# Routing by blocks of rows, and an output stored in two parts, in a graph and mixture-of-experts kernel

## The chip, the cores and the metric

One core of a Trainium2 chip. The number is device time in microseconds of one execution, start to end. The kernel before was run three times: 926.48, 929.12 and 930.1 us, median 929.12. All profile rows come from one more execution, with the profiler on.

## The reference

625 rows of 768 numbers pass two graph convolutions, then one transformer layer whose feed-forward part is a mixture of 8 experts, of which each row uses its best. All in float32. The part that this change touches, cut down:

```
x2   = x + attention(...) @ Wp + bp
h2   = layernorm(x2) * g + b
gate_logits = h2 @ Wg                       # 625 x 8
w, sel = top_k(gate_logits, 1)              # softmax over one value: w = 1
hid  = relu(h2 @ W1[sel] + b1[sel])         # 768 -> 3072
y    = hid @ W2[sel] + b2[sel]              # 3072 -> 768
out  = x_in + (x2 + w * y)
```

## The kernel before

**Rows and slots.** The 625 rows stand as C = 5 blocks of P = 125 rows on the partitions. Each expert takes CAP = 128 slots; a row's slot is 128 times its expert plus its rank among the rows of that expert (`own`), where rank is a count of the rows before it with the same choice. Rows beyond the 128 of an expert go to overflow tiles (`far`, `kk`, `home`, `over`), which a loop at the end runs if there are any.

**Precision.** Each float32 operand is split in a high part, written by ScalarE (`split_hi`, tile `whi`; helper line L599), and a low part, the difference, written by VectorE (`split_lo`, tile `wlo`; helper line L894). A product is three products.

**Weights.** W1 and W2 of an expert come in SCH = 16 chunks of 1152 KB: FCH = 8 of W1, 8 of W2. SyncE loads them into RAWS = 4 buffers `raw`; a buffer is free once the low part of its chunk is made. `whi`/`wlo` have SLOTS = 4 buffers, free once TensorE has used the chunk (`s_used`).

**The router.** For each block c: TensorE projects (`rows_product`), VectorE adds the residual (x2) and norms (n2), TensorE transposes n2, ScalarE scales it to h2T, TensorE makes the 8 gate products (L1596). The gates of block c-2 are made behind the projection of block c. When all five are there (`s_gate`), VectorE works on all blocks at once: best gate and its index, one-hot marks `ohb`/`ohe` (L1158 to L1173); TensorE counts ranks and totals with 20 small products (L1619, L1622); VectorE, having made the low part of chunk 0 ahead of that, computes `own`, the marks `oh0` of expert 0's rows (L1206), then slots and overflow tables (up to L1228). TensorE picks expert 0's rows with 60 products of marks and n2 into PSUM (L1639). ScalarE scales them (`hgf`, L819) and makes `hgh`, VectorE `hgl`, and the first expert starts. `keep_busy` issues products whose result nobody reads, 24, 24, 50 and 24 of them here.

**Tokens by DMA.** POOL scatters the five blocks of n2 to `hs_d` in DRAM by their slots (L548), then loads each expert's 128 rows one expert ahead (`next_in`, L554). Expert 0's own rows don't take this way. `hTT`, the hidden layer turned, lies over n2, so in expert 0 ScalarE and VectorE wait for the scatters at k = 7 (k - 2 = OVER_N2).

**One expert** (`tile`, chunks k = 0 to 15): products of W1 (L1675), ScalarE reads them (`hid`), TensorE transposes them, VectorE adds b1 (`bia`, L1258), ScalarE and VectorE make the two parts of relu (`hTT`); then products of W2 (L1694) into PSUM banks 4 and 5. At W2 chunk 1 the next expert's rows are transposed. Each expert's y is copied to `ysb` and POOL stores it to `ys_d` (L559).

**The last expert and the end.** The rows of experts 0 to 6 come back from `ys_d` with five gathers (`y_back`, L563), issued when TensorE has used 10 chunks of the last expert, and are added to `base` (L1279). The last expert's y takes no DMA: its marks `oh7T` and the one-hot choice `oh8T` were transposed in expert 0 (`marks_turned`); TensorE adds b2 by products with `oh8T` (`bias_y`, L1710) and spreads the split y over the rows with `oh7T` (`spread_y`, L1715), VectorE adds each block (L1289), and SyncE stores it (L456).

**Order.** All five engines run lists written out by hand; what stands behind a waiting instruction of an engine waits with it.

## Time and profile before

| what | value |
|---|---|
| median of three runs | 929.12 us |
| the profiled execution | 930.92 us |
| its span, first to last instruction | 929.4 us |
| TensorE busy | 874.0 us, 94% of the span |
| VectorE busy | 705.7 us, 76% |
| ScalarE busy | 556.4 us, 60% |
| POOL busy | 90.3 us, 10% |
| moved by DMA | 196.01 MB, 211 GB/s over the span |

The span runs from the first to the last instruction; the profiled execution's own time is 1.52 us more. Busy shares are averages over stages with different limits, so the stages are read by windows. Times inside the trace count from the span's start. In the chain of waits each line is a piece of work that the end depended on.

### The profile page before, as it was taken

What the parts mean: (1) busy time and instruction counts of PE and PEld (TensorE: products, weight loads), DVE (VectorE), ACT (ScalarE), POOL (GpSimd) and SP (SyncE); (2) the same over time, 40 slices, a digit from 0 to 9 for tenths busy, and PEclk for the clock granted to TensorE, in tenths of its full rate; (3) what the DMA queues carried; (4) which work ended last, traced back from release to release, by engine and by line L of the source; (5) the groups of instructions that cost most, each with busy time, mean ns of one, the idle gap of its engine ahead of it and who ended that gap; (6) DMA issues with size and microseconds to landing.
All of it is one profiled execution on the core that took longest, in us unless ns stands there. A gap on an engine that the chain in (4) does not pass through costs nothing.

```text
span 929.4 us, 14804 instructions
## 1 busy us (share of the span) xinstructions
PE 874.0 (94%) x5460; PEld 842.0 (91%) x5460; DVE 705.7 (76%) x1060; ACT 556.4 (60%) x780; POOL 90.3 (10%) x88
## 2 busy tenths in 40 slices
PE   7999898989998888899889999999999999999998
PEld 7899897989998667689889989999999999999996
DVE  7997155784333899855559889898998989898895
ACT  5503223154323788842548778787887878787870
POOL 2000006031000400012050000000000000000041
PEclk9999788999999999999799999999999999999998
DMA  7020006348114910060189999999999999999984
GB/s 228 3 101 1 1 2 119 85 101 183 55 51 112 326 71 2 1 185 1 36 254 327 331 349 354 376 335 377 363 361 377 354 378 344 379 358 368 369 288 130
DMA packets 116008, 196.01 MB, mean 211 GB/s; under 512 B 33828, under 2 KB 83196, under 8 KB 115958
## 3 DMA queue, kind: packets, MB, share of 16 engines
q1 hardware_dynamic: 107796, 169.08, 54.7%
q0 software_dynamic: 6336, 24.19, 7.8%
q10 hardware_dynamic: 1826, 2.06, 0.8%
q8 instruction: 33, 0.54, 0.2%
q14 instruction: 17, 0.14, 0.0%
HBM read 177.40 MB, written 17.90 MB: 210 GB/s over the span
## 4 chain that ended last, share of the span: by engine, by line
PE 43%; DVE 29%; DMA 13%; issue 7%; ACT 7%; SPq 0%; DVEq 0%; ACTq 0%
DVE wlo L894 14%; PE ps L1323 13%; DMA raw<-in_L_ffn_W 12%; PE ps L1499 7%; PE ps L1675 5%; PE ps L1694 5%; ACT whi L599 3%; DVE pr L1094 2%; DVE hTT L892 2%; DVE pTl L894 2%; PE ps L1352 1%; PE ps L1559 1%; DVE pr L1101 1%; DVE ohs L945 1%; DMA xs<-in_x 1%
## 5 line engine op out<-in xcount | busy, mean ns | idle before, releaser
L894 DVE TENSOR_TENSOR wlo<-raw,whi 128x2304 fp32r<-128x2304 f32 x137 | 350.9, 2570 | 23.7 <-ACT whi L599 23.5
L599 ACT ACTIVATE whi<-raw 128x2304 fp32r<-128x2304 f32 x139 | 296.2, 2132 | 83.4 <-DMA raw<-in_L_ffn_W 34.3
L1694 PE MATMUL ps<-whi,hTT 128*128 128x384 f32 x768 | 201.6, 339 | 1.0 <-ACT oh7T L599 1.0
L1694 PEld LDWEIGHTS ps<-whi,hTT 128*128 128x128 f32 x768 | 139.2, 188 | 1.2 <-ACT oh7T L599 1.2
L1675 PE MATMUL ps<-whi,hgh 128*128 128x384 f32 x384 | 134.1, 349 | 2.8 <-DVE hgl L894 2.8
L1675 PE MATMUL ps<-whi,hgl 128*128 128x384 f32 x384 | 130.3, 339 | 0.0
L1675 PE MATMUL ps<-wlo,hgh 128*128 128x384 f32 x384 | 129.8, 338 | 0.0
L1694 PE MATMUL ps<-wlo,hTT 128*128 128x384 f32 x384 | 129.0, 336 | 0.0
L1675 PEld LDWEIGHTS ps<-whi,hgh 128*128 128x128 f32 x384 | 73.3, 191 | 2.9 <-DVE hgl L894 2.9
L1675 PEld LDWEIGHTS ps<-wlo,hgh 128*128 128x128 f32 x384 | 73.2, 191 | 0.0
L1675 PEld LDWEIGHTS ps<-whi,hgl 128*128 128x128 f32 x384 | 73.0, 190 | 0.0
L1694 PEld LDWEIGHTS ps<-wlo,hTT 128*128 128x128 f32 x384 | 72.3, 188 | 0.0
L1352 PE MATMUL ps<-ohd,ohs 125*125 125x314 bf16 x400 | 58.2, 304 | 7.7 <-DVE ohd L946 5.7
L1352 PEld LDWEIGHTS ps<-ohd,ohs 125*125 125x125 bf16 x400 | 53.8, 139 | 10.9 <-DVE ohd L946 9.0
L1258 DVE TENSOR_TENSOR bia<-ps,b1T 128x384 f32<-128x384 f32 x64 | 35.6, 556 | 16.2 <-PE ps L1662 16.2
L606 ACT ACTIVATE root<-var 125x2 f32<-125x2 f32 (+2 forms) x13 | 2.7, 204 | 67.0 <-DVE var L914 66.9
L894 DVE TENSOR_TENSOR ql<-ps,qh 64x125 fp32r<-64x125 f32 (+1 forms) x66 | 21.8, 331 | 26.5 <-ACT qh L599 25.4
L1536 PE MATMUL ps<-ident,pr 125*125 125x125 f32 x168 | 30.6, 300 | 12.1 <-DVE pr L1101 7.6
L1536 PEld LDWEIGHTS ps<-ident,pr 125*125 125x125 f32 x168 | 22.4, 189 | 20.5 <-DVE pr L1101 9.5
L892 DVE SCALAR_TENSOR_TENSOR hTT<-bia,hTT 128x384 fp32r<-128x384 f32 x64 | 35.5, 554 | 5.6 <-ACT hTT L599 5.6
L599 ACT ACTIVATE qh<-ps 64x125 fp32r<-64x125 f32 (+1 forms) x66 | 20.1, 305 | 31.9 <-PE ps L1499 23.0
L756 ACT ACTIVATE pr<-pr,negmax 125x126 f32<-125x126 f32 (+4 forms) x60 | 36.0, 600 | 2.2 <-DVE negmax L1094 1.5
(282 smaller groups left out, 1761.6 us busy)
## 6 DMA issues: line engine op xcount, KB each, us to landing
raw<-in_L_ffn_W SPq DMA_DIRECT2D x128, 1152.0 KB, 6.9
hs_d<-bc POOLq DMA_DIRECT2D x13, 384.0 KB, 6.3
raw<-in_L_gnn_W SPq DMA_DIRECT2D x4, 1152.0 KB, 6.4
hs<-hs_d POOLq DMA_DIRECT2D x8, 384.0 KB, 5.6
ys_d<-ysb POOLq DMA_DIRECT2D x7, 384.0 KB, 6.0
raw<-in_L_ffn_Wv SPq DMA_DIRECT2D x6, 384.0 KB, 5.8
raw<-in_L_ffn_Wq SPq DMA_DIRECT2D x6, 384.0 KB, 5.2
raw<-in_L_ffn_Wk SPq DMA_DIRECT2D x6, 384.0 KB, 6.0
```

What stands on the lines that cost most here:

```text
L599: act.activation(out_, in_, func).then_inc(s, 1)
L756: act.activation(pr[:, u % PRS, 0:n], pr[:, u % PRS, 0:n], ACT.Exp, bias=negmax[:, u % 4, :], scale=-1.0, accum_out=ssum[:, u // 2 % 2, u ...
L892: dve.scalar_tensor_tensor(out_, in_, 0.0, hi_, ALU.max, ALU.subtract).then_inc(s, 1)
L894: dve.tensor_tensor(out_, in_, hi_, ALU.subtract).then_inc(s, 1)
L1094: dve.tensor_tensor_reduce(pr[:, u % PRS, 0:n], score_rows(u)[:, 0:n], cmask[:, (C - 1 - c) * P:(C - 1 - c) * P + n], -(float(D) ** -0.5), ...
L1258: dve.tensor_tensor(bia[:, k % 2, :, :], blocks(2 + k % 2, 128, JW, CAP), bcol.rearrange("p (j o) -> p j o", o=1).broadcast_to((128, JW, C ...
L1323: ins = mm(ps[0:P, bank + half, 0:HB], l, rr, start=m == 0 and i == 0, stop=m == DC - 1 and i == 2)
L1352: ins = mm(ps[0:P, m, 0:HALF], ohs[:, i % EU, m * P:(m + 1) * P], ohd[:, i % EU, :], start=i in BOUNDS, stop=i + 1 in BOUNDS)
L1499: ins = mm(ps[:, 2 * (m % 2) + half, 0:HALF], l, rr, start=c == 0 and i == 0, stop=c == DC - 1 and i == 2)
L1536: ins = nc.tensor.transpose(turned_part(u)[:, b, :], pr[:, u % PRS, b * P:(b + 1) * P], ident[0:P, 0:P])
L1675: ins = mm(ps[0:CAP, k % 2, 0:FW], l, rr, start=m == 0 and j == 0, stop=m == DC - 1 and j == 2)
L1694: ins = mm(ps[0:CAP, 4 + half, 0:HB], l, rr, start=k == 0 and j == 0 and jj == 0, stop=k == FCH - 1 and j == JW - 1 and jj == 2)
```

## The change

What it does:

- *Router by blocks.* Gates, choice, ranks and marks of block c are made as soon as that block is ready, in the gaps of the others (`chosen`, `placed`, `ranks`, `choice`). The gates of block c-2 stand in the middle of the projection of block c. Expert 0's rows are picked block by block, in six separate banks, and go through ScalarE and VectorE in halves. The fillers are 40, 8 and 30. On ScalarE h2T of block c-1 comes before the root of block c, and split 0 before the last h2T.
- *Later steps.* Totals, overflow tables and slots come behind the first two splits; `slot1`, `slot2`, the exponential and the overflow counts at k = 10 of expert 0.
- *b2 by gathers.* POOL gathers each row's b2 from DRAM into `x2` (three gathers before the scatters of n2, two behind), VectorE adds it to `base` at k = 11 to 15 of expert 0. The transposed marks and the bias products are gone.
- *The output in two parts.* In expert 0, `base` of the last expert's rows is scattered into 128 slots (`bs_d`; the others' index is out of bounds and skipped) and loaded into `bc[1]`; small products with the marks give each slot's row number and weight (`last_rows`). Gathers of y start after 8 chunks of the last expert. SyncE stores all blocks without the last expert's y. At the end VectorE makes y * w + base for the 128 slots, and one indirect DMA writes them over their rows in the output; empty slots are skipped.

The diff, cut (semaphores, tensors and the overflow branch are left out):

```diff
-Y_BACK_AT = 10
+Y_BACK_AT = 8
-TURN_BUSY = 24
-CHOICE_BUSY = 50
+NORM_BUSY = 40
+GATE_BUSY = 8
+SPLIT_BUSY = 30
...
@@ sync
-                sp.wait_ge(s_fin, c + 1)
+                sp.wait_ge(s_yin, c + 1)
...
@@ gpsimd
+            def bias_rows(c):
+                g.wait_ge(s_oh8, 2 * c + 1)
+                g.wait_ge(s_n2, c + 1)
+                g.wait_ge(s_base, c + 1)
+                g.indirect_dma_start(out=x2[:, c, :], out_offset=None, in_=b2[:, :],
+                                     in_offset=bass.IndirectOffsetOnAxis(ap=eidx[:, c:c + 1], axis=0)
+                                     ).then_inc(s_b2g[c], 16)
+            for c in range(C):
+                g.wait_ge(s_x2, c + 1)
+                gp.tensor_tensor(base[:, c, :], base[:, c, :], x2[:, c, :], ALU.add).then_inc(s_base, 1)
+                if c >= 2:
+                    bias_rows(c - 2)
...
             g.wait_ge(s_scat, 16 * C)
             next_in(0)
+            g.wait_ge(s_slot7, 1)
+            for c in range(C):
+                g.wait_ge(s_base2, c + 1)
+                g.indirect_dma_start(out=bs_d[:, :], out_offset=bass.IndirectOffsetOnAxis(ap=slot7[:, c:c + 1], axis=0),
+                                     in_=base[:, c, :], in_offset=None, bounds_check=CAP - 1, oob_is_err=False
+                                     ).then_inc(s_b7sc, 16)
+            g.wait_ge(s_b7sc, 16 * C)
+            g.dma_start(bc[1][0:CAP, :], bs_d[:, :]).then_inc(s_b7, 16)
...
+            g.wait_ge(s_row7, 1)
+            g.wait_ge(s_out, 32 * C)
+            g.wait_ge(s_y7, 2)
+            g.indirect_dma_start(out=out[:, :], out_offset=bass.IndirectOffsetOnAxis(ap=row7[:, 0:1], axis=0),
+                                 in_=ysb[0:CAP, :], in_offset=None, bounds_check=N - 1, oob_is_err=False
+                                 ).then_inc(s_out7, 16)
...
@@ vector
+            normed_rows(0)
+            normed_rows(1)
+            chosen(0)
+            normed_rows(2)
+            chosen(1)
+            normed_rows(3)
+            chosen(2)
+            normed_rows(4)
+            d.wait_ge(s_iotac, 1)
+            placed(0, 3)
+            chosen(3)
+            placed(3, 4)
+            chosen(4)
+            placed(4, 5)
             split_lo(0, 0)
+            for i, part in enumerate((slice(0, HALF_IN), slice(HALF_IN, DC))):
+                d.wait_ge(s_hgh, i + 1)
+                lo(hg[1][:, part, :], hgf[:, part, :], hg[0][:, part, :], s_hgl)
+            split_lo(1, 0)
+            d.wait_ge(s_rank, C + 1)
...
+                    if first and k == FCH + 2:
+                        for c in range(C):
+                            dve.tensor_scalar(oh0[:, c, :], iotac[:, :], float(CAP * (E - 1)), home[:, c:c + 1],
+                                              ALU.add, ALU.is_equal).then_inc(s_ohe, 1)
...
+                    if first and FCH + 3 <= k < FCH + 3 + C:
+                        c = k - FCH - 3
+                        dve.scalar_tensor_tensor(base[:, c, :], x2[:, c, :], wtok[:, c:c + 1], base[:, c, :],
+                                                 ALU.mult, ALU.add).then_inc(s_base2, 1)
...
             for half in range(2):
...
-                lo(wlo[0][0:CAP, part], ps[0:CAP, 4 + half, 0:HB], whi[0][0:CAP, part], s_yl)
+                dve.scalar_tensor_tensor(ysb[0:CAP, part], ps[0:CAP, 4 + half, 0:HB], rowf[:, 1:2], bc[1][0:CAP, part],
+                                         ALU.mult, ALU.add).then_inc(s_y7, 1)
...
@@ tensor
-                rows_product(q, 2 * WP, c, 4 + 2 * (c % 2), None if c else {DC - 1: (s_pvl, 2 * STEPS)}).then_inc(s_wp, 1)
-                if c >= 2:
-                    gate_products(c - 2)
+                rows_product(q, 2 * WP, c, 4 + 2 * (c % 2), None if c else {DC - 1: (s_pvl, 2 * STEPS)},
+                             (lambda b=c - 2: gate_products(b)) if c >= 2 else None).then_inc(s_wp, 1)
                 if c >= 1:
                     turn_n2(c - 1)
+                if c >= 2:
+                    ranks(c - 2)
+            pe.wait_ge(s_x2, 4)
+            busy(NORM_BUSY, 7)
+            gate_products(3)
+            turn_n2(4)
+            busy(GATE_BUSY, 7)
+            pe.wait_ge(s_x2, C)
+            choice(0, range(2, DC))
+            ranks(3)
+            choice(1, range(2, DC))
+            gate_products(4)
+            choice(2, range(2, DC))
+            for c in range(3):
+                choice(c, range(2))
+            ranks(4)
...
+            choice(3, range(DC))
+            choice(4, range(DC)).then_inc(s_hgT, 1)
+            pe.wait_ge(s_rkread, C)
+            busy(SPLIT_BUSY, 3)
...
-                    if first and k == 1:
-                        marks_turned()
-                if first:
-                    pe.wait_ge(s_ohl, 2)
-                else:
+                if not first:
                     pe.wait_ge(s_yev, 2 * t)
...
-            def bias_y(c, half):
...
-            def spread_y(c, half):
```

## Rows read from the trace of the kernel before

**Rows 1.** windows of three stretches: length, PE, PEld, DVE, ACT, POOL busy, clock, DMA
```profile
449.50:452.50 3.00, 2.03 (x18) 1.94 (x18) 0.00 (x0) 2.14 (x7) 0.00 (x0) 1.00 0.00 0
452.50:455.00 2.50, 2.40 (x13) 2.40 (x13) 0.00 (x0) 2.48 (x3) 0.00 (x0) 0.56 0.00 0
...
535.00:545.00 10.00, 8.12 (x40) 7.80 (x39) 7.50 (x4) 7.04 (x5) 0.54 (x1) 0.83 1.04 376
...
655.00:709.00 54.00, 53.85 (x322) 53.25 (x321) 49.24 (x35) 43.80 (x42) 1.08 (x2) 1.00 1.03 364
```

**Rows 2.** chain of waits: start us, length us, what ran
```profile
...
475.22 8.09 PE ps L1675 x36
...
531.42 6.96 DMA raw<-in_L_ffn_W
...
541.51 4.71 PE ps L1675 x18
...
895.22 18.72 PE ps L1694 x108
...
```

**Rows 3.** timeline of TensorE in the router: start, length, operation
```profile
...
444.38 1.37 PE L1596 MATMUL ps<-wg,h2T 128*125 128x8 f32 x12
...
464.14 6.92 PE L1639 MATMUL ps<-oh,n 125*128 125x128 f32 x60
...
```

**Rows 4.** timeline of VectorE in the router
```profile
...
444.58 0.96 DVE L1146 TENSOR_TENSOR x<-ps,xfb 125x768 f32<-125x768 f32 x1 [4.05 <-PE ps L1323]
...
448.08 0.68 DVE L931 TENSOR_SCALAR n<-x,mv,rstd 125x768 f32<-125x768 f32 x1
...
461.35 1.07 DVE L1206 TENSOR_SCALAR oh<-iotac,rt 125x128 f32<-125x128 f32 x5
...
463.93 0.17 DVE L1217 CAST slot<-rt 125x5 int32<-125x5 f32 x1
...
465.09 5.01 DVE L894 TENSOR_TENSOR wlo<-raw,whi 128x2304 fp32r<-128x2304 f32 x2
...
```

**Rows 5.** timeline of ScalarE in the router
```profile
...
471.10 2.20 ACT L819 ACTIVATE hgf<-ps,lnT 128x128 f32<-128x128 f32 x6 [9.58 <-PE ps L1639]
473.33 0.84 ACT L599 ACTIVATE hgh<-hgf 128x768 fp32r<-128x768 f32 x1
...
```

**Rows 6.** timeline of SyncE, first weights after the router
```profile
...
460.48 18.70 SPq L442 DMA_DIRECT2D raw<-in_L_ffn_W  x4
...
```

**Rows 7.** timeline of VectorE in W1 chunks of a later expert
```profile
...
659.53 2.55 DVE L894 TENSOR_TENSOR wlo<-raw,whi 128x2304 fp32r<-128x2304 f32 x1
...
662.93 2.55 DVE L894 TENSOR_TENSOR wlo<-raw,whi 128x2304 fp32r<-128x2304 f32 x1
...
```

**Rows 8.** timeline of VectorE at the end
```profile
...
906.14 0.95 DVE L894 TENSOR_TENSOR hgl<-hgf,hgh 128x768 fp32r<-128x768 f32 x1
...
924.82 1.02 DVE L1289 SCALAR_TENSOR_TENSOR base<-ps,wtok,base 125x768 f32<-125x768 f32 x1 [1.54 <-PE ps L1715]
...
```

**Rows 9.** timeline of POOL behind the router and at the end
```profile
...
465.10 6.15 POOL L548 DMA_INDIRECT hs_d<-n,slot  x1 [17.48 <-DVE slot L1217]
...
476.52 3.31 POOL L548 DMA_INDIRECT hs_d<-n,slot  x1 [0.30 <-issue]
489.36 0.61 POOL L554 DMA_DIRECT2D hs<-hs_d  x1 [9.53 <-DMA hs_d<-n,slot]
...
895.59 3.08 POOL L563 DMA_INDIRECT x<-ys_d,slot  x1 [33.60 <-issue]
...
907.61 1.20 POOL L563 DMA_INDIRECT x<-ys_d,slot  x1 [0.31 <-issue]
...
```

**Rows 10.** page, costliest groups: busy, mean ns, idle before and its releaser
```profile
...
L1694 PE MATMUL ps<-whi,hTT 128*128 128x384 f32 x768 | 201.6, 339 | 1.0 <-ACT oh7T L599 1.0
...
```

**Rows 11.** landing of DMAs touching hs_d, then of the gathers into x2
```profile
DMA to landing us min/median/max: 2.7/6.3/12.6
...
DMA to landing us min/median/max: 6.6/7.9/8.5
```

More of the change, by code:

```diff
@@ L571, in _ @@
                 y_out(t)
[L572 removed]
+            g.wait_ge(s_base2, C)
             g.wait_ge(s_route, 1)
@@ L843, in tile @@
                         y_read(t)
-                    if k + AHEAD < SCH and not (first and k == 0):
+                    if k + AHEAD < SCH:
                         split_hi(k + AHEAD, t)
@@ new lines, in placed @@
+            def placed(c0, c1):
+                d.wait_ge(s_rank, c1)
+                d.wait_ge(s_oh8, 2 * c1)
+                dve.tensor_tensor(prod[:, c0:c1, :], rank8[:, c0:c1, :], ohe[:, c0:c1, :], ALU.mult
+                                  ).then_inc(s_rkread, c1 - c0)
+                d.wait_ge(s_rkread, c1)
+                step(dve.reduce_sum(rank[:, c0:c1], prod[:, c0:c1, :], AX))
+                step(dve.scalar_tensor_tensor(own[:, c0:c1], ef5[:, c0:c1], float(CAP), rank[:, c0:c1],
+                                              ALU.mult, ALU.add))
+                for c in range(c0, c1):
+                    dve.tensor_scalar(oh0[:, c, :], iotac[:, :], own[:, c:c + 1], None, ALU.is_equal).then_inc(s_oh0, 1)
@@ L1260, in tile @@
                                           ALU.add).then_inc(s_bia, 1)
-                    if k + 2 < SCH and not (first and k < 2):
+                    if k + 2 < SCH:
                         split_lo(k + 2, t)
@@ L1597, in gate_products, with ranks, choice, busy @@
                              start=m == 0, stop=m == DC - 1)
-                return ins
+                ins.then_inc(s_gate, 1)
+            ohb = rt[:, 4, 0:C * E // 2].bitcast(BF16).rearrange("p (c e) -> p c e", e=E)
+            def ranks(c):
+                pe.wait_ge(s_oh8, 2 * c + 1)
+                if c >= 3:
+                    pe.wait_ge(s_rkread, c)
+                for b in range(c + 1):
+                    ins = mm(ps[0:P, 3, c * E:(c + 1) * E], before[:, :] if b == c else onesb[:, :], ohb[:, b, :],
+                             start=b == 0, stop=b == c)
+                ins.then_inc(s_rank, 1)
+            def choice(c, part):
+                pe.wait_ge(s_oh0, c + 1)
+                for m in part:
+                    ins = mm(first_in(m), n2[:, c, m * 128:(m + 1) * 128], oh0[:, c, :], start=c == 0, stop=c == C - 1)
+                return ins
+            def busy(n, bank):
+                keep_busy(n, onesb[:, :], onesb[:, :], bank)
             pe.wait_ge(s_wg, 16)
```

322 lines of the change are left out of this document (152 added, 170 removed).

## The prediction

> **What bounds the kernel now.** I read the page first: TensorE is busy 94% of the span (the table above), so time can only come out of stretches where it works without need, waits, or runs at its lower clock. The table of windows finds them. Between 655 and 709 us one expert fills TensorE (53.85 of 54.00 us) while the DMA engines are busy too (364 GB/s), VectorE 49.2: a balanced stage which this change doesn't shorten. Around 450 to 475 it is different: TensorE is busy 2.03 of 3.00 us, and in the next 2.50 us its granted clock is 0.56, nearly the lower of its levels, 1.2 in place of 2.4 GHz [rows 1]. There the router works. The chain of waits shows three places: the router up to the first expert product at 475.22, waits on weight transfers around the start of expert 1 (one of 6.96 us; one group of 18 products at 541.51 takes 4.71 us where 3.13 is usual), and, from the last expert product's end (895.22 + 18.72 = 913.94) to 929.4, a tail of 15.5 us [rows 2].
>
> **The change, part by part.**
>
> *Router.* In before, the last block's projection ends at 444.4 and the experts start at 475.22: 30.8 us [rows 2, 3]. New chain, from the same moment. One gate group of 1.37 us [rows 3] now stands inside the last projection, and three tiny rank products before it (estimate 0.5): projection ends 446.2. x2 and norm take 4.2 (444.58 to 448.76); ScalarE now does six h2T (2.2 us, as its six of 471.10 in the same form) before the root, which holds it back an estimated 0.4: n2 of the last block ready at 451.0 [rows 4, 5]. Meanwhile TensorE does 40 fillers and gates of block 3, then the six transposes: 452.5. h2T 2.2 (the first whi split, 2.15, now fits ahead of it): 454.7. Gate products 1.4: 456.1 [rows 3, 5]. VectorE picks one block in six small steps of about 0.2: 457.5. Five rank products 0.6, then product, sum, own, one mark: 0.9, at 459.0. Choice products are 6.92/60 = 0.115 each; 24 to 36 of the 60 (blocks 0 to 2) are done in the gaps, the last 12 cost 1.4: 460.3 [rows 3]. ScalarE's half of the tile is half of 2.20 + 0.84, so 1.5: 461.8; VectorE's half 0.5: 462.3 [rows 4, 5]. With semaphore gaps I take 463.0, **12.2 us earlier**. Gone are the totals' arithmetic before the marks, the five marks in a row (1.07), the split of chunk 0 standing ahead of the rank reading (2.55) and most of the 50 fillers. Bounds: 462.3, if the clock stays up; 466, if gates, ranks and choices run at 1.2 GHz as the gates of 452.5 to 455 did [rows 1]. Fewer and shorter pauses speak for the full clock; I take nothing for it but 0.7.
>
> *Given back in expert 0.* The move of work past VectorE's queue has a price. Split 0 now ends at 461.6, about 1.1 later than the first weight issue shows in before (460.48) [rows 6]. Split 1 (2.55) follows the tile's lower half, at 466.4; the ten steps up to `slot` (about 2.1) follow; splits 2 and 3 end at 471.0 and 473.5. Chunk 1 then starts 0.8 late and chunk 2 1.2 late: **+2.0**. In the first eight chunks VectorE has a split of 2.55 and two instructions of half a us, overlapping a little, every 3.4 us, all that TensorE's pace leaves, so it regains nothing [rows 7]. Behind k = 10 come 5 marks and some 17 small steps, 3.5 us (0.17 each and half as much between dependent ones; five marks took 1.07 [rows 4]); at k = 12 four steps, 0.8; at k = 11 to 15 five base adds of 1.0 [rows 8]: 9.4 us. VectorE's slack in W2 chunks is 3.12 - 2.55 = 0.6 each, and it comes in with a lead of about one. Step by step: split 12 ends 505.2, then 3.5 of marks; split 13 511.3, chunk 13 wants it at 510.6 (0.7); split 14 514.9 (0.5 more); split 15 519.3 (1.3); expert 1's first split 525.9 (3.5). Net TensorE waits **+6.0**. Bounds: 1 (VectorE's lead is a full ring, about 5 us) and 9.4.
>
> *Scatter of tokens.* `slot` is ready at 468.4, not 464.1. I read the POOL rows against VectorE's: the issue of 895.59 ends at 898.67 and that of 476.52 at 479.83, each 1.1 us behind the end of a `wlo` split, while 471.56 and 907.61, with VectorE idle, take 1.2; the first, 6.15 us, ended 1.1 us behind a pair of splits without a gap [rows 4, 9]. In the new place VectorE splits every 3.4 us, so five issues end about 485, and 5.4 to 9.5 us later (from 479.83 to 489.36 it was 9.5) the rows have landed: 490 to 494. ScalarE waits for them at k = 7, which is now at about 491; the hid read behind that wait holds TensorE: **+1.5**, bounds 0 and 5. The three b2 gathers ahead of it lie beside the norms and cost nothing; if POOL were not free by 468 they'd delay the scatter, but each has 8 us. The base scatter and its load come at 505 to 530, and POOL's next work is the y of expert 0, stored after its end: hidden.
> The Trainium skill ("SBUF — State Buffer", Who interferes with whom) says that a VectorE tensor_tensor with both inputs in SBUF blocks GpSimd's reads for the whole instruction; the rows agree. The same skill ("GPSIMD Engine Reference", Instruction dispatch) would put the 6.15 us down to a code load of about 6 us at a first call; then the b2 gather would pay it, the scatters would end about 3 us sooner, and the +1.5 would be 0. The ends 1.1 us behind splits fit the first rule better.
>
> *Taken out of expert 0 and 1.* Ten transposes of marks (1.1), the wait for oh7T at the first W2 chunk (1.0 [rows 10]) and two ScalarE copies; one of the 1.7 us that chunks 0 and 1 took longer (36 in 8.09 where 6.3 is usual), since 30 fillers now bridge the gap ahead; and the waits on transfers with the low clock in them at 535 to 545, 1.9 idle and 1.7 [rows 1, 2]: TensorE now waits for VectorE in that place instead, and a later TensorE finds the weights there. Together **-6.7**.
>
> Last expert product's end: 913.9 - 12.2 + 2.0 + 6.0 + 1.5 - 6.7 = **904.5**. From expert 2 on nothing moves but the start.
>
> *Tail.* Gone: 20 bias products, 20 spread products, the splits of y, five final adds and the stores behind the last of them (924.82 + 1.02 to 929.4: 3.6) [rows 8]. Gathers start at chunk 8 of the last expert, 8 x 3.12 = 25 us before its end instead of 18.3; at 3.1 to 3.4 an issue the last ends 9.4 before the end and lands about 5.4 later [rows 9, 11], so at -4. VectorE's adds go from -6.8 (906.14 + 0.95 in before) to -1.9, SyncE's stores follow, the last lands 3.6 later: **+1.7**, so the stores don't quite hide. POOL's last scatter waits for them; y of half 1 is ready at +0.8 (0.25 + 0.5). Then 0.3 for POOL, 1.2 to issue (VectorE idle), landing: plain POOL stores show 2.7, the quickest gather 6.6, both from the issue's start [rows 11]; 78 of 125 rows, nothing beside it: 4.7. Tail 1.7 + 0.3 + 4.7 = 6.7, with the drain 7.0 instead of 15.5: **-8.5**. Bounds: 4.7 and 1.7 + 0.3 + 12.6 = 14.6 (the slowest landing).
> The Trainium skill ("DMA: Bandwidth & Descriptors", Anatomy of one DMA) fits a POOL DMA as 2.0 us plus bytes over 436 GB/s, an estimate of 2.6 for 0.24 MB; by it the tail would be nearer 5.
>
> Span 904.5 + 7.0 = 911.5. The profiled execution took 930.92 for a span of 929.4, so 913.0; the median of the runs shown is 1.8 below that execution. Forecast **912** (rounded up from 911.2 for the gaps between small steps).
>
> **Rivals.**
> A. *Weights set the end* (11 in 100). 124 transfers of 1152 KB come after the first freed buffer, at 350 to 365 GB/s where TensorE needs 350. If their stream has no slack, what counts is the first split, which is 1.1 us later: end at 915.0, tail 7.0, span 922.0, time **922**. For it: waits on `raw` in experts 0 and 1. Against: from 655 on TensorE has none.
> B. *The tail isn't shortened* (9 in 100): gathers that contend with the last weights, stores and then a dependent scatter in series, 15 us together as now. 904.5 + 15.5: **920**. For it: the +1.7 above; against: nothing else uses the DMA engines then.
> C. *POOL is kept out by VectorE* (5 in 100), the slower side. If each issue misses every gap as the first did, 6.15 + 0.3: token scatters end at 502, land at 508 or later, expert 0 stands 15 us instead of 1.5 (end at 918); the five gathers end at +7, land at +12.4, stores at +17, the last scatter at +29: span 947, time **947**. It decides from about 4.2 us an issue. Against: of the ten issues only that one missed a gap between two splits.
> D. *No move*: VectorE's added 9.4 falls whole on TensorE, clock at 1.2 GHz in the router, scatter +5: 904.5 + 3.4 + 3 + 3.5 = 914.4, tail 12, span 926.4: **926** (3 in 100).
>
> **How the numbers follow.** Forecast 72 in 100, its own range 904 to 919. A and B reach 922; D and C lie outside. Range 904 to 925. A measurement of this kernel tells a change from 0.5%, 4.6 us: faster means below 924.5. That holds the forecast, A and B: 0.91; same 0.04; slower 0.05.
>
> **What would show it.** First expert product at 463 (over 467: the router's sum fails). The third product group of expert 1 at 531 to 533 where it now is 541.51; waits on `wlo` in chunks 13 to 16. Token scatter issues each ending 1.1 behind a split. A tail of 7 with the last store landing just behind the last product. Wrong if the last expert product ends later than 910, or the tail is over 11.

## The result, and the profile after

The changed kernel takes **941.85 us** (median of 4 runs, 939.01 to 944.81); the kernel before takes 929.24 beside it. The ratio is **1.0141** (95% interval 1.0109 to 1.0174): 12.6 us slower. Forecast were 912 us and a range of 904 to 925. The profiled execution took 942.54 us for a span of 940.6.

The last projection before the router ends somewhere between 440 and 451 us, differently in each execution of either kernel. So all stages below are counted from that moment, with the kernel before beside the forecast (which had it at 446.2) and the measurement:

| us from the last projection's end | before | forecast | after |
|---|---|---|---|
| the projection's end itself, from the span's start | 444.4 | 446.2 | 446.5 |
| first product of expert 0, W1 | 30.9 | 16.8 | 17.6 |
| expert 0, W2 | 62.2 | | 62.5 |
| expert 1, W1 | 88.3 | | 92.9 |
| expert 2, W1 | 145.3 | | 152.5 |
| end of the last expert product | 469.6 | 458.3 | 476.9 |
| from there to the span's end | 15.5 | 7.0 | 17.2 |

The table is read to about 0.2 us. The two kernels' last projection doesn't hold quite the same work: in after the gate products of one block stand inside it (it takes 7.9 us, 6.6 before), which before has behind it. From one and the same moment the router is therefore some 12 us shorter, not 13.3, and the last product comes some 8.6 us later, not 7.3.

The router came out as worked out. Of its gain nothing was left at W2 of expert 0; 7 more were lost until expert 2 and nothing behind it (324.3 us from there to the last product before, 324.4 after), and the tail got longer, not shorter.

The page of after, its costliest groups (busy, mean ns, idle before and its releaser). ScalarE's idle time ahead of its split stood at 83.4 us before, 34.3 of it by `raw`:

```profile
L648 ACT ACTIVATE whi<-raw 128x2304 fp32r<-128x2304 f32 x139 | 296.2, 2133 | 105.1 <-DMA raw<-in_L_ffn_W 57.8
...
L1776 PE MATMUL ps<-ident,hid 128*128 128x128 f32 x192 | 32.7, 280 | 17.1 <-ACT hid L904 17.1
```

The windows of after (columns as in [rows 1]):

```profile
452.50:455.00 2.50, 2.49 (x26) 2.30 (x24) 1.76 (x11) 2.50 (x7) 0.00 (x0) 1.00 0.25 102
455.00:465.00 10.00, 9.35 (x100) 9.21 (x100) 4.96 (x14) 6.48 (x10) 0.00 (x0) 1.00 0.20 40
485.00:495.00 10.00, 6.07 (x30) 5.72 (x28) 4.96 (x5) 5.83 (x6) 3.33 (x3) 0.83 1.04 359
495.00:505.00 10.00, 7.02 (x41) 6.38 (x39) 6.52 (x5) 2.92 (x3) 0.51 (x1) 1.00 1.03 263
505.00:515.00 10.00, 6.53 (x32) 6.50 (x33) 5.16 (x6) 8.66 (x9) 0.00 (x0) 0.83 0.82 292
535.00:545.00 10.00, 8.38 (x48) 8.07 (x48) 10.00 (x7) 4.76 (x3) 9.39 (x3) 1.00 0.82 265
655.00:709.00 54.00, 54.00 (x322) 53.70 (x321) 49.56 (x35) 43.95 (x41) 1.12 (x3) 1.00 1.03 365
```

The first line answers to the 0.56 of [rows 1]: the clock now stays up through the router. The next to read are 485 to 515, with the same three windows of before:

```profile
485.00:495.00 10.00, 10.00 (x63) 9.90 (x62) 8.97 (x8) 7.30 (x10) 0.61 (x1) 1.00 0.81 274
495.00:505.00 10.00, 10.00 (x61) 9.76 (x60) 10.00 (x9) 8.16 (x9) 0.00 (x0) 1.00 0.98 353
505.00:515.00 10.00, 9.01 (x56) 8.65 (x56) 8.79 (x9) 8.41 (x9) 0.19 (x1) 1.00 0.92 303
```

In after TensorE works 6 to 7 of 10 us there, where it worked 9 to 10, and VectorE has time to spare too, while the DMA engines are full until 505. What is missing is weights. With the pauses the granted clock falls to 0.83 in two of the three windows. At 535 to 545 it is VectorE that is full. From 655 on the two kernels are alike.

The chain of waits of after, against [rows 2]:

```profile
465.72 2.47 DVE wlo L941
...
473.01 6.38 DMA raw<-in_L_ffn_W
...
485.93 19.90 DMA raw<-in_L_ffn_W
...
519.84 0.98 DVE oh L1319 x5
...
525.68 0.93 DVE base L1354
...
539.43 7.07 DMA raw<-in_L_ffn_W
...
549.98 4.28 PE ps L1791 x18
554.59 3.15 PE ps L1791 x18
...
910.04 9.76 DMA x<-ys_d,slot
...
927.46 3.28 DMA out_x<-base
```

One transfer of weights is on the chain for 19.90 us. The group of 18 products that was slow at 541.51 is still slow, at 549.98: what I had counted as gone only moved. GpSimd's timeline and, below it, the transfers issued from 470 to 512 (KB each, median us from issue to landing):

```profile
471.49 2.58 POOL L573 DMA_INDIRECT hs_d<-n,slot  x1 [20.66 <-DVE slot L1285]
...
483.15 1.19 POOL L573 DMA_INDIRECT hs_d<-n,slot  x1 [0.30 <-issue]
484.64 2.36 POOL L560 DMA_INDIRECT x<-in_L_ffn_b,eidx  x1 [0.30 <-issue]
487.31 1.22 POOL L560 DMA_INDIRECT x<-in_L_ffn_b,eidx  x1 [0.31 <-issue]
494.89 0.63 POOL L581 DMA_DIRECT2D hs<-hs_d  x1 [6.36 <-DMA hs_d<-n,slot]
```
```profile
raw<-in_L_ffn_W SPq DMA_DIRECT2D x8, 1152.0 KB, 12.9
...
hs_d<-n,slot POOLq DMA_INDIRECT x5, 11.5
x<-in_L_ffn_b,eidx POOLq DMA_INDIRECT x2, 16.9
```

In the same window of the kernel before the weights' median is 7.7 us. Last, the end of after: VectorE, GpSimd, the sequencers' last instructions (ns, then start), and one window:

```profile
925.34 1.14 DVE L1376 SCALAR_TENSOR_TENSOR ysb<-ps,rowf,bc 128x384 f32<-128x384 f32 x2
931.76 1.02 POOL L618 DMA_INDIRECT out_x<-ysb,row  x1 [18.78 <-issue]
```
```profile
L88 POOLq DRAIN  x1: 5461/5461/5461, 934.9 to 934.9; - x1
L88 SPq DRAIN  x1: 7/7/7, 935.0 to 935.0; - x1
```
```profile
936.00:938.00 2.00, 0.00 (x0) 0.00 (x0) 0.00 (x0) 0.00 (x0) 0.00 (x0) 0.50 0.00 0
```

The scatter that I had worked out at 4.7 us lands 3.0 us behind its issue, but then GpSimd's DRAIN, the last thing of its program, takes 5.46 us, and the span ends 0.2 us behind it. In the kernel before the same instruction took 4.48 us at 915.3, beside the last products and adds.

### The profile page after: what moved, and what is told of

Read it like the earlier page. It is cut to its first block, busy times and chain, and to the rows that moved or that the text cites. A ratio compares the mean times of both kernels' runs of the same rounds, so it can differ in the third digit from the quotient of the medians.

```text
span 940.6 us, 14716 instructions
## 1 busy us (share of the span) xinstructions
PE 861.8 (92%) x5376; PEld 831.3 (88%) x5376; DVE 709.9 (75%) x1097; ACT 553.7 (59%) x776; POOL 118.3 (13%) x101
## 4 chain that ended last, share of the span: by engine, by line
PE 59%; DVE 19%; DMA 10%; ACT 5%; issue 5%; POOL 1%; SPq 0%; DVEq 0%; POOLq 0%; ACTq 0%
PE ps L1791 14%; PE ps L1412 13%; PE ps L1806 11%; DMA raw<-in_L_ffn_W 7%; DVE wlo L941 7%; PE ps L1588 7%; PE ps L1441 3%; PE ps L1776 2%; DVE pr L1141 2%; PE ps L1648 2%; DVE pTl L941 2%; DMA xs<-in_x 1%; POOL x L590 1%; PE ps L1625 1%; DVE pr L1148 1%
## 5 line engine op out<-in xcount | busy, mean ns | idle before, releaser
L1806 PE MATMUL ps<-whi,hTT 128*128 128x384 f32 x768 | 204.4, 342 | 0.3 <-DVE wlo L941 0.3
L1776 PE MATMUL ps<-ident,hid 128*128 128x128 f32 x192 | 32.7, 280 | 17.1 <-ACT hid L904 17.1
L1776 PEld LDWEIGHTS ps<-ident,hid 128*128 128x128 f32 x192 | 24.5, 143 | 22.2 <-ACT hid L904 20.3
L1625 PE MATMUL ps<-ident,pr 125*125 125x125 f32 x168 | 31.1, 305 | 11.3 <-DVE pr L1148 8.0
```

The lines of the kernel that those rows point to most:

```text
L1625: ins = nc.tensor.transpose(turned_part(u)[:, b, :], pr[:, u % PRS, b * P:(b + 1) * P], ident[0:P, 0:P])
L1776: ins = nc.tensor.transpose(blocks(2 + k % 2, 128, JW, CAP)[:, j, :], hid[0:CAP, k % 2, j * 128:(j + 1) * 128], ident[0:CAP, 0:CAP])
L1806: ins = mm(ps[0:CAP, 4 + half, 0:HB], l, rr, start=k == 0 and j == 0 and jj == 0, stop=k == FCH - 1 and j == JW - 1 and jj == 2)
```

## The experiments

"Stage" means us from the last projection's end to W1 of expert 1, to W1 of expert 2 and to the end of the last product; "tail" what follows that. After: stage 92.9, 152.5, 476.9, tail 17.2. Before: 88.3, 145.3, 469.6, tail 15.5. Ratios are to the kernel before on the same chip, with their 95% intervals.

How much a single profile tells: after and the four kernels that change only its end (tail_nobranch, tail_plain, tail_nowait, tail_early) have the same code up to the last expert. Their stages run from 90.7 to 93.3 at expert 1 and from 149.5 to 153.0 at expert 2, and the four with the same last expert end it at 474.7 to 478.1. So a difference of two profiles is good to about 3 us.

### What the transfers of GpSimd cost in expert 0

**b2_early**: the two gathers move ahead of the scatters.
```
             for c in range(C):
                 gp.tensor_tensor(base[:, c, :], ...)
                 if c >= 2: bias_rows(c - 2)
+            for c in range(C - 2, C): bias_rows(c)
             ...                       # five scatters to hs_d
-            for c in range(C - 2, C): bias_rows(c)
```


> The b2 gathers of blocks 3 and 4 are issued ahead of the token scatters, at about 455 to 460, when no weights are under way. Theory 1 (POOL's DMAs and the weights share the DMA engines in the first half of expert 0): 0.77 MB leave the stretch in which weight transfers take 12 to 20 us; the first W2 product of expert 0 (509.4 in the changed kernel) comes at 503 to 506, time 5 us lower (937). Theory 2 (the weights are late by themselves, and what costs is that ScalarE's read of hid stands behind a split that waits for them): under 1.5 us.

934.45 us, ratio 1.0093 (1.0056 to 1.013); stage 85.2, 143.6, 468.9, tail 17.7. Two gathers in another place give 7.9 us (7.4 in the times), 7.7 of it by expert 1. In their new place the DMA engines had been busy for 0.18 to 0.25 of the time. From 470 to 512:
```profile
raw<-in_L_ffn_W SPq DMA_DIRECT2D x10, 1152.0 KB, 8.6
```

**no_pool_dma**: all five b2 gathers and the five token scatters left out of after; experts 1 to 7 then work on zeros, and b2 is missing.
```
-                g.indirect_dma_start(out=hs_d[:, :], ..., in_=n2[:, c, :], ...)   # x5
-                bias_rows(...)                                                    # x5
```


> Leaves out the token scatters (experts 1 to 7 work on zeros) and all b2 gathers (b2 is left out), with the waits on them. Theory 1: weight transfers of expert 0 take 6 to 8 us, no wait on them in its first half, first W2 product at 492 to 495 as the prediction had it, time 14 to 16 us lower (927). Theory 2: still late, above 503. Theory 3 (VectorE's added work) says that whatever is won there, expert 0's second half still gives back about 6 us.

929.25 us, 1.0039 (1.0009 to 1.0069); stage 79.4, 137.4, 462.0. Without them 8.9 of the router's 13.3 us arrive at expert 1, and 7.6 are there at the last product. ScalarE's waits for `raw` in W1 of expert 0 are 7.5 us here, 13.7 in b2_early, 21.7 in after and 1.8 before. The run takes out gathers and scatters together; the scatters alone were not left out.

**hid_first**: in expert 0 ScalarE reads the product first and splits the chunk three ahead behind it.
```
-                    if k + AHEAD < SCH: split_hi(k + AHEAD, t)
+                    if k + AHEAD < SCH and not first: split_hi(k + AHEAD, t)
                     ...                                  # hid read, hTT
+                    if first and k + AHEAD < SCH: split_hi(k + AHEAD, t)
```


> In expert 0 alone, ScalarE reads hid and makes hTT before the split of the chunk three ahead, which may wait for its transfer. Theory 2: TensorE no longer stands at the hid transposes (12.3 us between 464 and 512 in the changed kernel), first W2 product of expert 0 at 500 to 503, time 6 to 9 us lower. Theory 1: TensorE waits for the same chunks a little later, under 2 us.

940.0 us, 1.0152 (1.0115 to 1.019). W2 of expert 0 begins 11 us sooner (51.6 for 62.5), and W1 of expert 1 only 3.7, little more than two profiles can tell apart. The time can't be told from that of after: the wait for `hid` was mostly the form in which late weights reached TensorE.

**slots_early**: the ten small steps up to `slot` stand ahead of the tile's lower half, and the first scatter is issued 0.5 us behind the first product, not 7.3.
```
             split_lo(0, 0)
+            ...                                          # totals to slot
             for i, part in enumerate(...): lo(hg[1]...)
             split_lo(1, 0)
-            ...                                          # totals to slot
```


> The totals and the slots are computed between split 0 and the tile's lower half, so the token scatters start at 465 instead of 471.5; the first expert product comes 0.9 us later. Theory 1: part of the scatters is over before TensorE needs chunk 5, first W2 product of expert 0 at 504, time 4 to 5 us lower. Theory 2: 0.9 us slower.

941.15 us, 1.0171 (1.01 to 1.0242); stage 91.4, 151.3, 476.2. No gain that shows: moved 7 us ahead against the first product, the scatters cost what they cost before.

**before_b2** and **before_plain**: the same two gathers, or two plain loads of as many bytes, in the kernel before.
```
             ...                                          # before's token scatters
+            for c in range(C - 2, C):
+                g.indirect_dma_start(out=x2[:, c, :], in_=b2[:, :], in_offset=...eidx...)
+                # its twin: g.dma_start(x2[:, c, :], tok(xf_d)[:, c, :])
```


> The kernel before with only two gathers of b2 rows (768 KB together) added behind its token scatters, into a buffer that nothing reads until the end. Theory T1 by bytes: 0.77 MB at 360 GB/s takes 2.1 us from a weight stream without slack, so expert 1 starts 2 us later and the time is 929 to 930 against 927.4. Theory T1 by rows (a gather that reads the same eight rows over and over is slower than its bytes): 5 to 7 us, 932 to 934. Rival T5 (before has slack that hides it, and what the kernel after lost came from its earlier start alone): no change, 927 to 928.

> The twin of the run with two b2 gathers in the kernel before: the same 768 KB in the same place, as two plain loads of different rows. By bytes: 929 to 930, like its twin. By rows: 929 to 930 here against 932 to 934 for the twin. Slack hides it: 927 to 928 both.

929.47 us, 1.0054 (1.0025 to 1.0082), and 926.03, 0.9998 (0.9974 to 1.0022). The kernel before hides the plain loads wholly; the gathers cost it 0.3 to 0.8%, and less than the 7.9 us that they cost the kernel after. Their intervals don't overlap, but their profiles lie 0.6 us apart at the last product, and that of before_b2 (924.96 us) is the second fastest of its nine runs; that eight rows read over and over are slower is likely, not shown.

### The lead of the weights

**held_10**: 160 more fillers on TensorE ahead of the first product.
```
-            busy(SPLIT_BUSY, 3)
+            busy(SPLIT_BUSY + 160, 3)
```


> The kernel after with 160 more of the fillers of 0.064 us on TensorE between the choice of the first tile and the first expert product: TensorE starts the experts 10 us later, as late as in the kernel before, and everything else keeps its order. Theory L (the weight stream sets expert 0: its first refill waits for VectorE's first split, which came at 460.5 in the kernel before and comes at 461.6 in the kernel after, so an earlier first product only used up the 14.7 us by which the stream was ahead): the first product moves from 464 to 474, but expert 1's start (539.4) moves by 3 us at most, and the time is 942 to 945. Rival M (the start of TensorE counts one for one and the losses in expert 0 come from elsewhere): expert 1 starts at 549, and the time is 951 to 953.

941.49 us, 1.0167 (1.0103 to 1.0232); first product 26.1, stage 96.1, 156.4, 480.8. The first product comes 8.5 us later than in the five kernels with the same code. W1 of expert 1 comes 2.8 to 5.4 us later than theirs (3.2 against after, 5.4 against tail_plain), the last product 2.7 to 6.1 later than in four of them, and the time can't be told from that of after. So of a start held back by 8.5 us between a third and two thirds costs nothing. M, one for one, is ruled out; L had said 3 us at most, which these profiles can't decide.

**split_early** (on b2_early): the splits of chunks 0 and 1 go into gaps of VectorE in the router.
```
             placed(3, 4)
+            split_lo(0, 0)
             chosen(4)
             placed(4, 5)
-            split_lo(0, 0)
+            split_lo(1, 0)
             for i, part in enumerate(...): lo(hg[1]...)
-            split_lo(1, 0)
```


> On top of the version with the b2 gathers ahead of the token scatters (934.5): VectorE's low splits of chunks 0 and 1 stand ahead of the last block's choice and right behind its marks, in gaps where VectorE waits for the router, in place of behind the marks and behind the tile's halves; slot then comes 2.5 us sooner. Theory L (the stream sets expert 0): the first refill goes out 4 to 5 us earlier, the second 6, and expert 0's W2 starts 4 to 6 us earlier against the first product (38.1 us between them there, 32 to 34 then), with up to 1 us lost at the first product; the time is 929 to 931. Rival T1 (the token scatters alone hold the stream back, whenever it starts): W2 stays 37 to 38 us behind the first product and the time 934 to 935.

929.96 us, 1.0038 (1.0011 to 1.0065); stage 82.3, 140.8, 465.1, tail 17.5. The first refill goes out 7.0 us ahead of the first product, not 2.1; that product comes at 18.0 as ever, and W2 of expert 0 34.4 behind it, not 38.1. As theory L has it, and the best version measured that leaves nothing out. The 3.8 us at the last product are near what two profiles can tell; best_tail, which shares this change, shows 2.7 there, and the times differ by 4.5 with intervals that overlap a little.

### VectorE's added work

**base_off** (on b2_early): base adds and base scatters left out; b2 and the base of the last expert's rows are missing from the output.
```
-                        dve.scalar_tensor_tensor(base[:, c, :], x2..., wtok..., base...)   # x5
-                g.indirect_dma_start(out=bs_d[:, :], ..., in_=base[:, c, :], ...)          # x5
```


> On top of the version with the b2 gathers ahead of the token scatters (934.5 us): the five base adds that VectorE does in expert 0 and the five scatters of base rows are left out, so the output lacks its b2 term and the last expert's rows lack their base. Theory T3 (VectorE's added work at chunks 13 to 16, and the base scatters beside it, hold TensorE around expert 1's start): that start of W1 (531.51 there) comes 4 to 6 us earlier against the first product of expert 0's W2 (29.4 us between them now, 25 to 26 then, the 26.1 of the kernel before), and the time is 934.5 - 5 = 929 to 930. Rival T1b (weights alone are late there, since the stream has no slack left once expert 0 has used it up): the W2 phase stays 28.5 to 29.5 us and the time 933 to 934.

927.49 us, 1.0029 (0.9995 to 1.0064); stage 81.7, 137.8, 463.7: 5.3 us for the two together.

**no_base_scatter** (on split_early): only the five scatters left out, so the last expert's rows lack their base.


> The version with b2 gathers ahead and two early splits (930.0), its five base adds kept and the five base scatters left out, so the last expert's rows lack their base. Theory V (VectorE's adds are what costs): 929 to 930, and 465 us from the last projection's end to the last expert product, as there. Rival S (the scatters' issues and their 1.9 MB cost): 925 to 926, 460 to 461 us. Leaving out both had given 5.3 us.

934.6 us, 1.0085 (1.0059 to 1.0111); stage 83.7, 144.5, 475.5, tail 15.0. No gain, so it is likely the adds that cost and not the scatters; the adds alone were not left out. Why it came out slower than the version with them stays open. Its profile has more waits for weights around expert 1's first chunks, with the clock at 0.66 from 535 to 545, and its last expert takes 60.8 us where split_early's takes 54.0: TensorE stands idle for 4.25 us ahead of its last chunk, whose transfer took 15.7 us.

**base_late** (on split_early): adds and scatters in expert 3.
```
-            with d.Fori(1, E) as t: tile(t, t)
+            with d.Fori(1, 3) as t: tile(t, t)
+            tile(3, 3, sums=True)
+            with d.Fori(4, E) as t: tile(t, t)
```


> On top of the version with the two early splits (930.0): the five base adds and base scatters, and the load behind them, stand in expert 3 in place of expert 0. Theory T3-moment (experts 0 and 1 have no lead in weights, and later experts have one that takes up VectorE's 5 us and 1.9 MB of scatters): 4 to 5 us better, 925 to 926; from the last projection's end to the last expert product 460 to 461 us where it was 465.1. Rival T3-work (the same work costs the same in any expert): 930, and 465.

931.78 us, 1.0042 (1.0016 to 1.0068); stage 79.8, 135.9, 465.0. At expert 2 it is 4.9 us ahead, at the end level. 3.7 of that go where the adds now are (from W1 of expert 4 to W1 of expert 5 it takes 57.4 us, 53.7 in split_early) and 1.0 in the last expert, where the two kernels don't differ: mostly rival T3-work. The chain shows where, at the end of expert 3:
```profile
689.99 1.64 DVE base L1356 x2
691.76 5.04 DVE wlo L944 x2
696.95 7.45 DMA raw<-in_L_ffn_W
```
A late split frees `raw` late, and the next transfer is late in turn.

**split_pool** (on split_early): the base adds on GpSimd, as a product and a sum.


> As the version with the two early splits, and the five base adds of expert 0 moved from VectorE to GpSimd (each as a product and a sum, in one row before its base scatter). Leaving adds and base scatters out gave 6 us (927.5 where the version with them had some 933 on the same scale). Theory T3 (VectorE's work there is what counts): 3 to 5 us better than the version with the two early splits alone, 925 to 927. Rival T3b (the base scatters' transfers, or GpSimd's use of the SBUF port against VectorE's splits, are what counts): no gain, within 1 us of it, or slower.

944.16 us, 1.0193 (1.0125 to 1.0262); stage 84.4, 154.7, 480.4, 14 us worse. GpSimd's sum, 1.81 us in the router, takes 4.04 beside VectorE's splits:
```profile
512.28 3.64 POOL L602 TENSOR_TENSOR x<-x,wtok 125x768 f32<-125x768 f32 x1 [19.82 <-DVE tokw L1350]
516.00 4.04 POOL L605 TENSOR_TENSOR base<-base,x 125x768 f32<-125x768 f32 x1
```
The splits get longer too: two that take 5.02 together took 7.92 at 526.32. The Trainium skill ("SBUF — State Buffer", Who interferes with whom) has a VectorE instruction with two SBUF inputs contend with a GpSimd instruction that reads SBUF; the trace agrees, and here both get longer. But most of the 14 us is something else. GpSimd is busy with adds and base scatters until 562, and the load of the next expert's rows stands behind them in its list. It goes out at 570.47, at 541.75 in split_early, and TensorE waits for it in expert 1, which takes 70.3 us in place of 58.6:
```profile
578.15 1.54 PE L1755 MATMUL ps<-ident,hs 128*128 128x128 f32 x6 [6.66 <-DMA hs<-hs_d]
```
So this run doesn't tell what the adds would be worth on an engine with time to spare.

### The tail

**tail_nobranch**: GpSimd's branch for overflow rows left out. **tail_plain**: a plain store to a scratch tensor, on the same queue, in place of the last scatter; the last expert's rows are missing. **tail_nowait**: GpSimd's own wait for the last scatter gone (SyncE's stays).
```
-            n_over = g.value_load(...); with g.If(n_over > 0): ...      # tail_nobranch
-            g.indirect_dma_start(out=out[:, :], ..., in_=ysb[0:CAP, :])  # tail_plain
+            g.dma_start(bs_d[:, :], ysb[0:CAP, :])
-            g.wait_ge(s_out7, 16)                                        # tail_nowait
```


> The kernel after without GpSimd's branch for overflow experts behind the last scatter (the path that handles overflow rows is left out on GpSimd; there are none in this input). In the trace of after the last scatter's rows land at 934.8 and nothing moves until the span ends at 940.6: 5.8 us. Theory E (GpSimd, which waits for the scatter after a register load and a jump over the branch, spends these 5.8 us getting there): the span ends within 1.5 us of the landing, so the time is 942 - 4.5 = 937 to 938. Rival F (the scatter's completion itself reaches the waiting engines this late, whatever stands behind it): 941 to 942, and the empty stretch stays 5 to 6 us.

> The kernel after with the last scatter replaced by a plain store of the same rows, from the same queue and behind the same waits, to a scratch tensor: the last expert's rows are missing from the output. The scatter's last bytes move 3.0 us after its issue, and the span ends 5.8 us later. Theory F1 (the scatter by indices completes late): with a plain store the span ends within 2 us of the last bytes, 4 to 5 us sooner, 937 to 938. Rival F2 (every last transfer of GpSimd's queue costs that): the same 5 to 6 us of nothing, 941 to 942.

> The kernel after without GpSimd's own last wait for its scatter (SyncE waits for it anyway). In after the scatter is issued at 931.76 to 932.78, its last bytes move until 934.8, and the span ends at 940.6. Theory G (GpSimd's program takes some 6 us to end behind its last wait, whatever it waited for): the span then ends about 6 us behind the issue's end or 2 us sooner than in after, 15.2 us behind the last expert product where it was 17.2. Rival F (the completion comes late to every waiting engine): no change, 17 us.

936.35 us, 1.0122 (1.006 to 1.0183), tail 17.9; 937.36, 1.0134 (1.0064 to 1.0204), tail 16.7; 938.99, 1.0138 (1.0095 to 1.0181), tail 15.6. The times can't be told apart, the profiles can: neither branch nor kind of transfer matters, and with the wait gone the end comes 6.7 us behind the scatter's issue instead of 8.8. The row says what it is:
```profile
L88 POOLq DRAIN  x1: 5752/5752/5752, 932.6 to 932.6; - x1
```
It begins 0.3 us before the scatter's issue has ended, 2.2 ahead of the landing, and ends 5.5 us behind that issue. No run gives the last transfer to SyncE, so what the end costs without GpSimd's DRAIN is not measured.

**tail_early**: gathers of the other experts' rows from chunk 4 of the last expert on, VectorE's adds at its chunks 11 to 15.
```
-Y_BACK_AT = 8
+Y_BACK_AT = 4
+                    if last and 11 <= k < 11 + C: others_y(k - 11)
-            for c in range(C): others_y(c)                # behind the last expert
```


> The kernel after with its last expert written out on VectorE: the gathers of the other experts' rows start at chunk 4 (of 16) in place of 8, and VectorE's adds stand at chunks 11 to 15 in place of behind the last split. Theory H (the stores of out stand behind VectorE's adds and hold the last scatter back by 4 us): stores land within 1.5 us of the last product, the scatter is issued at +3, and the tail is 12 to 13 us in place of 17.2, time 937 to 938. Rival I (gathers and stores beside the last weights hold TensorE back by as much as the tail gets shorter): 941 to 943.

947.73 us, 1.0223 (1.0168 to 1.0278); last product 482.7, tail 15.0. Rival I, and worse: 2.2 us off the tail for 5.8 on the expert, whose last two transfers of weights took 15.0 and 18.5 us. **all_moved** puts split_early, base_late, tail_early and tail_nowait together:


> All edits together: b2 gathers ahead of the token scatters, splits of chunks 0 and 1 early, base adds and base scatters in expert 3, the early tail, GpSimd's last wait gone. If the causes add up: 930.0 - 4.5 (base late) - 4.5 (tail) - 2 (last wait) = 919, 7 us better than the kernel before. If the gathers at chunk 4 cost the last expert what the tail gives back, 923 to 925.

932.78 us, 1.007 (1.0045 to 1.0095); stage 80.6, 136.7, 476.1, tail **8.5**. At expert 2 it is 15.8 us ahead of after, and it has the short tail: VectorE's last add ends 3.2 us ahead of the last product, so the last scatter waits for y alone and goes out 1.6 behind that product. But 15 us are given back. From W1 of expert 4 to W1 of expert 5 it takes 59.1 us (53.7 in split_early; the base adds in expert 3), and the last expert takes 64.3 (54.3 in after), 10 where tail_early's gathers alone cost 6; the other 4 no run separates. **best_tail** (on split_early): out written by five scatters on GpSimd that skip the last expert's rows, so that the last scatter waits for no store.


> The version with b2 gathers ahead and two early splits, with another tail: out is written by five scatters on GpSimd that skip the last expert's rows, each behind its own add, so that the last scatter no longer waits for the stores; VectorE's adds stand ahead of the tile arithmetic that follows its last split; GpSimd doesn't wait for its last transfers. In that version the last scatter is issued 8.7 us behind the last expert product and the span ends 8.8 later. If the tail is what these waits say, the issue comes at +5 to +6, its end is +6 to +7, and GpSimd's program ends 5.7 later: tail 12 to 13 us in place of 17.5, time 925 to 926, level with the kernel before or 0.2% under it. If scatters of whole blocks land late (10 us and more), the tail stays 16 to 17 and the time 929 to 930.

933.48 us, 1.0082 (1.005 to 1.0114), tail 17.3. The last issue comes 7.9 us behind the last product (8.7 in split_early), and the DRAIN is twice as long:
```profile
920.48 1.02 POOL L620 DMA_INDIRECT out_x<-ysb,row  x1 [0.30 <-issue]
```
```profile
L88 POOLq DRAIN  x1: 11201/11201/11201, 918.5 to 918.5; - x1
```
Not all of that is cost: the record begins 3.0 us before the last of the six issues has ended. From that end it is 8.2 us, where tail_nowait, with one scatter and no wait, has 5.5; 1.8 of it lie behind the last landing. The stores were off the path, and issues and DRAIN of GpSimd took their place. No version beats the kernel before.

## Why the prediction was wrong, step by step

- **Router, -12.2**: right. 17.6 us from the last projection's end where 16.8 was forecast, and some 12 us in all; the clock held at 1.00.
- **Late splits, +2.0, and the -6.7 for waits that go**: here it failed, at the sentence "a later TensorE finds the weights there". I set TensorE's delay behind VectorE against the transfers and left out that it also started 11 us earlier against them. In the kernel before the first refill went out at 460.48, 14.7 us ahead of the first product; now it goes out at 462.11, 2.1 ahead. The forecast counted the split that frees `raw` as 1.1 us late and priced no consequence but two chunks. With the lead ScalarE waited 1.8 us for `raw` in expert 0's W1, without it 21.7, of which the next term has 8. That the lead was what hid the token scatters fits these waits; no run has the lead back with everything else as in after. split_early, which has 4.9 us more of it, is 3.8 us ahead of b2_early; held_10, which has 8.5 more by a later start, makes up between a third and two thirds of that delay.
- **b2 gathers, nothing**: costed for the three beside the norms; the two behind the token scatters were not costed at all ("each has 8 us" was said of GpSimd's time, not of the DMA engines'). b2_early measures 7.9 us: the largest single miss in the experts.
- **Token scatter, +1.5**: the place and the rule were right (the first four issues end at 474.07, 476.53, 479.45 and 482.84, each 1.1 us behind a split's end). ScalarE never came to wait for it first: the weights were later.
- **VectorE's additions, +6.0**: of the right kind, its size only in part tested. base_off measures 5.3 for the five base adds with their scatters, 5.0 of the 9.4 us of work in this term; the marks behind k = 10 show up at 519.84 on the chain, but no run leaves them out, so the whole may be more than 6. Expert 3 doesn't absorb the adds either (base_late).
- **Tail, -8.5**: wrong by 10.2, 17.2 where 7.0 was forecast. The first step that failed is "VectorE's adds go from -6.8". That was the end of VectorE's last split and the tile step behind it in the kernel before; in after it is -2.6. The gathers were nearly as forecast: the last landed at -3.6 (forecast -4). What was late is the last chunk of weights:
```profile
915.19 2.13 ACT L648 ACTIVATE whi<-raw 128x2304 fp32r<-128x2304 f32 x1 [5.19 <-DMA raw<-in_L_ffn_W]
```
```profile
917.35 2.56 DVE L941 TENSOR_TENSOR wlo<-raw,whi 128x2304 fp32r<-128x2304 f32 x1 [5.45 <-ACT whi L648]
919.83 0.95 DVE L941 TENSOR_TENSOR hgl<-hgf,hgh 128x768 fp32r<-128x768 f32 x1
920.70 4.73 DVE L1366 SCALAR_TENSOR_TENSOR base<-x,wtok,base 125x768 f32<-125x768 f32 x5
```
  Its transfer took 11.7 us beside the gathers that now start at chunk 8. The three kernels with gathers from chunk 10 on (before, before_b2, before_plain) have 5.4 to 5.6; the thirteen others with chunk 8 whose trace holds this transfer have 11.3 or more; tail_early, with chunk 4, has 18.5. So the adds ended at +2.0 (forecast -1.9), the last stores landed at +7.3 (forecast +1.7), and the scatter went out at +8.4. Then came 3.0 for landing (forecast 4.7) and 5.5 of GpSimd's DRAIN, for which the forecast had 0.3 of "drain". The early gathers, counted as pure gain, also held TensorE up by 0 to 1.4 us ahead of its last chunk.
- **The rivals**: A had the right mechanism, a stream without slack, and priced it at its own 1.1 us where its whole lead of 12 was gone. B had the gathers contend with the last weights, as they do, and the stores and the scatter in series; the DRAIN it had not. Both at once, plus the gathers, was no case of mine, and 5 in 100 for slower was far too sure. C was not seen where it was put: token scatters took 1.2 to 3.1 us to issue and the gathers of y 2.2 to 3.6. But two of the five base scatters, which the forecast called hidden, took 5.55 and 5.10. D summed side effects and still ended 14 us short of the span. The chances of the forecast, A and B add up to 92 in 100, not 91.

With the router's 13.3 us taken off the 469.6 of before, the last product would have come at 456.3; it came at 476.9. So 20.6 us were given back, where the forecast had 2.8. Undoing the parts one by one prices 17.0 of them: 7.9 (the gathers' place), 3.8 (the late splits) and 5.3 (base adds and base scatters). Each is a difference of two single profiles, and they were not undone all at once. The other 3.6 are not separated; the token scatters, now without a lead that hides them, are the candidate (no_pool_dma ends 6.9 us ahead of b2_early).

## What to carry to other kernels

Before you count an earlier start of the bound engine as gain, write down by how much the transfers feeding it run ahead now, and what that lead hides; if the edit moves the consumer and not the instruction that frees the buffer, it spends the lead. In a stage in which engine and DMA are both full, an extra vector instruction or transfer may cost its whole time, in a later repetition as in the first: the base adds cost about 5 us in expert 0 and 3.7 in expert 3, gathers brought forward doubled the time of the last weights' transfer, while plain loads of 768 KB in the kernel before cost nothing. And the engine that issues the last transfer puts the end of its own program on the path: look at its last instruction in the trace, even where something else covers it now.

## What the runs showed of the hardware that was not expected

- GpSimd's DRAIN at the program's end takes 4.48 us (before, its last transfer landed 1.1 us earlier) and 5.46 to 5.97 (one scatter or store just ahead), where SyncE's takes 0.01. In best_tail it is 11.20, of which 3.0 overlap the last issues.
- The first indirect DMA of the kernel after took 1.29 us to issue at 432.82. The Trainium skill ("GPSIMD Engine Reference", Instruction dispatch) would have a code load of about 6 us at a first call; this trace doesn't show it, and the 6.15 us of [rows 9] fits the pair of VectorE splits beside it.
- Two indirect gathers of 384 KB among five scatters took the weights' landing from 8.6 to 12.9 us in the median, with 359 GB/s moved at 485 to 495 and 263 in the ten us behind it.
- The last chunk's transfer of 1152 KB takes 5.5 us in before and 11.3 or more in the kernels whose five gathers of y start at chunk 8 of the last expert; TensorE's wait for it is up to 1.4 us, 4.25 in no_base_scatter.
